# A long convolution with plain float32 operands in place of three float32r products, four filter-tile slots and two input-row buffers

## What is computed

```python
K = 2.0 * jnp.einsum('hn,hnl->hl', Ct, jnp.exp(P)).real      # one filter per head
y = irfft(rfft(u, n=2*L) * rfft(K, n=2*L)[None], n=2*L)[..., :L] + u * D[:, None]
y = y * mask[:, None, :]
# feed-forward, every operand fake-quantised to 8 bits by its rows' maxima:
gate = qlinear(y, w_gate); up = qlinear(y, w_up)
out = x + qlinear(silu(gate) * up, w_down)
```

## Time and profile before

| | us |
|---|---|
| median of 2 runs | 1431.74 |
| lowest, highest | 1426.31, 1437.16 |
| profiled execution | 1423.75 |
| its span | 1422.0 |

### The profile page before, as it was taken

The page is one execution under the profiler, slowest core; times in us unless marked ns, Lnnn a source line. Parts: engine busy times, 40 slices in busy tenths (PEclk is TensorE's granted clock), DMA queues, the critical chain, the costliest instruction groups (busy, mean ns, idle before and its releaser), DMA issues.

```text
span 1422.0 us, 21733 instructions
## 1 busy us (share of the span) xinstructions
PE 1298.7 (91%) x7444; PEld 769.8 (54%) x7444; DVE 1000.0 (70%) x1617; ACT 466.8 (33%) x665; POOL 490.2 (34%) x343
## 2 busy tenths in 40 slices
PE   2378888888888799999999999999999999999998
PEld 0377777878878644444444444444444444444443
DVE  7658889798899766556765676567656765676565
ACT  1145555555565322222222222222222222222222
POOL 2257666676677411222122212221222121212220
PEclk9999999999999899999999999999999999999999
DMA  0087776777787422323322332233223322332222
GB/s 4 8 249 232 217 233 199 235 213 215 252 267 236 164 59 65 63 65 70 90 62 65 70 87 65 65 70 87 65 65 70 85 66 65 70 83 68 65 64 74
DMA packets 137599, 161.58 MB, mean 114 GB/s; under 512 B 101644, under 2 KB 101854, under 8 KB 136286
## 3 DMA queue, kind: packets, MB, share of 16 engines
q1 hardware_dynamic: 137566, 161.16, 40.9%
HBM read 113.28 MB, written 25.49 MB: 98 GB/s over the span
## 4 chain that ended last, share of the span: by engine, by line
PE 64%; DVE 0%; ACT 0%; issue 0%
PE ps_o L1113 22%; PE ps_g L1088 21%; PE ps_u L1088 21%; PE ps_t L1098 0%; ACT h_t L1216 0%; DVE ps_o L1168 0%; DVE res L1171 0%
## 5 line engine op out<-in xcount | busy, mean ns | idle before, releaser
L1242 POOL TENSOR_TENSOR h_int<-h,rounder 128x512 bf16<-128x512 f32 x186 | 186.7, 1025 | 698.2 <-ACT h L1207 695.5
L1088 PE MATMUL ps_g<-wgu,rows 128*128 128x512 bf16 (+1 forms) x1536 | 330.8, 359 | 4.5 <-PEq L377 4.5
L1088 PE MATMUL ps_u<-wgu,rows 128*128 128x512 bf16 (+1 forms) x1536 | 329.0, 357 | 0.0
L1113 PE MATMUL ps_o<-wd,h_t 128*128 128x512 bf16 (+1 forms) x1408 | 319.1, 380 | 0.0
L1201 ACT ACTIVATE g_buf<-g_buf 128x512 f32<-128x512 f32 x192 | 112.3, 585 | 596.3 <-DVE g_buf L1139 596.3
L1139 DVE SCALAR_TENSOR_TENSOR g_buf<-ps_g,sx_all,wide 128x512 f32<-128x512 f32 x192 | 132.3, 689 | 242.4 <-PE ps_g L1088 242.4
L1088 PEld LDWEIGHTS ps_g<-wgu,rows 128*128 128x128 bf16 x1536 | 145.0, 98 | 163.6 <-issue 13.2
L1113 PEld LDWEIGHTS ps_o<-wd,h_t 128*128 128x128 bf16 (+1 forms) x1408 | 134.2, 98 | 178.0 <-issue 34.4
L1088 PEld LDWEIGHTS ps_u<-wgu,rows 128*128 128x128 bf16 x1536 | 146.9, 98 | 151.6 <-issue 0.8
L611 POOL TENSOR_TENSOR t_lo<-t_raw,t_hi 128x1024 fp32r<-128x1024 f32 x64 | 162.5, 2540 | 81.2 <-ACT t_hi L657 81.2
L875 PE MATMUL ps_y<-u_hi,t_hi 128*128 128x512 f32 (+7 forms) x512 | 171.8, 336 | 8.1 <-POOL t_lo L611 3.5
(11 more groups left out here) (149 smaller groups left out, 1024.5 us busy)
## 6 DMA issues: line engine op xcount, KB each, us to landing
t_raw<-k_rev SPq DMA_DIRECT2D x64, 512.0 KB, 5.9
rows<-in_x SPq DMA_DIRECT2D x64, 256.0 KB, 3.9
res<-in_x SPq DMA_DIRECT2D x64, 256.0 KB, 3.9
out_x<-res SPq DMA_DIRECT2D x64, 256.0 KB, 3.2
wide<-in_L_ffn_w_gate SPq DMA_DIRECT2D x22, 512.0 KB, 6.2
wide<-in_L_ffn_w_up SPq DMA_DIRECT2D x22, 512.0 KB, 7.4
wide<-in_L_ffn_w_down SPq DMA_DIRECT2D x8, 1376.0 KB, 7.6
xq_dram<-xq SPq DMA_DIRECT2D x32, 256.0 KB, 5.8
```

Of the source, the lines that this page charges most:

```text
L1088: last = pe.matmul(bank[:, 0:n], xq[:, par, c, :], wgu[:, NC - 1 - c, first + cols.start:first + cols.stop], start=(c == 0), stop=(c == NC ...
L1113: last = pe.matmul(ps_o[o][:], h_t[0:width, c, :], wd[0:width, c, o * W:(o + 1) * W], start=(c == 0), stop=(c == FC - 1))
L1242: pool.tensor_tensor(h_int[:, piece(j)], h[:, par, piece(j)], rounder[:].to_broadcast([P, n]), ALU.subtract).then_inc(h_int_ready, 1)
```

## The change

The operands of the convolution become plain float32: one matmul for each block instead of three, 8 for a head instead of 24, straight from the loaded filter tile `toep` and from the turned input `u`. The splits (`t_high`, `split_t`, `u_low`) and their semaphores are gone; `u_high` becomes `take_u`, the same ScalarE copy out of PSUM into a float32 tile. The filter tiles get four slots (two tiles x two heads) and the input rows a second buffer, so SyncE loads two tiles ahead: filter tile (i+2, hh) is loaded once `convolve(i, hh)` is done, input rows i+2 once tile i has been turned. The first loads are reordered: input rows first, then the filter tiles, and all of tile 1 without a wait.

```diff
-        t_raw = sb("t_raw", [P, 2, L])
-        t_hi = sb("t_hi", [P, 2, L], F32R)
-        t_lo = sb("t_lo", [P, 2, L], F32R)
-        u_hi = sb("u_hi", [P, 2, NC * B], F32R)
-        u_lo = sb("u_lo", [P, 2, NC * B], F32R)
+        toep = sb("toep", [P, 4, L])
+        u = sb("u", [P, 2, NC * B])
+        x_more = sb("x_more", [P, L])
+        x_bufs = (x_rows, x_more)
...
-            load_t(0, 0)
-            load_x(0)
-            load_t(0, 1)
-            for i in range(2):
-                for u in range(2):
-                    load_gu(i, i, u)
-            sp.wait_ge(x_turned, 2)
-            load_x(1)
+            load_x(0, 0)
+            load_t(0, 0, 0)
+            load_t(0, 0, 1)
+            for g in range(2):
+                load_gu(0, 0, g)
+            load_x(1, 1)
+            for g in range(2):
+                load_gu(1, 1, g)
             for hh in range(2):
-                sp.wait_ge(t_lo_done, hh + 1)
-                load_t(1, hh)
+                load_t(1, 1, hh)
...
-                    sp.wait_ge(x_turned, 2 * i + 4)
-                    load_x(i + 2)
-
-                    sp.wait_ge(t_lo_done, 2 * i + 3)
-                    load_t(i + 2, 0)
+                    sp.wait_ge(x_turned, 2 * i + 2)
+                    load_x(i + 2, par)
+
+                    sp.wait_ge(conv_done, 2 * i + 1)
+                    load_t(i + 2, par, 0)
...
-            split_t(0, 0)
-            split_t(0, 1)
...
-                    t_high(i + 1, 0)
-                    u_high(i + 1, 0)
+                    take_u(i + 1, 0)
...
-                if has(i, TILES - 1):
-                    u_low(i + 1, 0)
...
-                pe.wait_ge(x_loaded, 32 * i + 32)
-                pe.wait_ge(u_lo_done, 2 * i + hh - 1)
+            def await_x(i, par):
+                pe.wait_ge(x_loaded[par], 16 * i - 16 * par + 32)
...
-                    parts = ((t_hi, u_hi), (t_hi, u_lo), (t_lo, u_hi))
-                    for k, (t, u) in enumerate(parts):
-                        last = pe.matmul(out[:, dist * B:NC * B], t[:, hh, block_cols], u[:, hh, 0:n],
-                                         start=(dist == 0 and k == 0), stop=(dist == NC - 1 and k == 2),
-                                         skip_group_check=True)
+                    last = pe.matmul(out[:, dist * B:NC * B], toep[:, slot, block_cols], u[:, hh, 0:n],
+                                     start=(dist == 0), stop=(dist == NC - 1), skip_group_check=True)
```

More of the change, by code:

```diff
@@ L507, in _, with load_t, load_x @@
         def _(sp):
-            def load_t(i, hh):
+            def load_t(i, par, hh):
+                slot = 2 * par + hh
                 src = bass.AP(tensor=k_rev.tensor, offset=(2 * i + hh) * KROW, ap=[[1, P], [1, L]])
-                sp.dma_start(t_raw[:, hh, :], src).then_inc(t_loaded[hh], 16)
-            def load_x(i):
+                sp.dma_start(toep[:, slot, :], src).then_inc(t_loaded[slot], 16)
+            def load_x(i, par):
                 for hh in range(2):
-                    sp.dma_start(x_rows[hh * B:(hh + 1) * B, :],
-                                 x[:, bass.ds(2 * i + hh, 1), :].squeeze(1)).then_inc(x_loaded, 16)
+                    sp.dma_start(x_bufs[par][hh * B:(hh + 1) * B, :],
+                                 x[:, bass.ds(2 * i + hh, 1), :].squeeze(1)).then_inc(x_loaded[par], 16)
             def load_gu(i, par, u):
@@ L608, in _ @@
         def _(pool):
[L609 to L612, removed]
             def unround(i, par, k, turned):
@@ L643, in body @@
                     unround(i + 1, 1 - par, 0, pieces(i, 0) + 1)
-                if has(i, TILES - 1):
-                    split_t(i + 1, 1)
                 if not gate_stage(i) and has(i, WEIGHT_ITERS - 1):
@@ L652, in _, with take_u @@
         def _(act):
-            def t_high(i, hh):
-                act.wait_ge(t_loaded[hh], 16 * i + 16)
-                if not isinstance(i, int) or i >= 1:
-                    act.wait_ge(conv_done, 2 * i + hh - 1)
-                act.activation(t_hi[:, hh, :], t_raw[:, hh, :], ACT.Copy).then_inc(t_hi_done, 1)
-            def u_high(i, hh):
+            def take_u(i, hh):
                 act.wait_ge(x_turned, 2 * i + hh + 1)
@@ L694, in _ @@
             for hh in range(2):
-                t_high(0, hh)
-                u_high(0, hh)
+                take_u(0, hh)
             round_gu(0, 0, 0)
@@ L720, in body @@
                 if has(i, TILES - 1):
-                    t_high(i + 1, 1)
-                    u_high(i + 1, 1)
+                    take_u(i + 1, 1)
                 if gate_stage(i):
@@ L776, in scale_w @@
                 dve.wait_ge(w_step, 3 * turn + 3)
-            def u_low(i, hh):
-                dve.wait_ge(u_hi_done, 2 * i + hh + 1)
-                dve.tensor_tensor(u_lo[:, hh, :], ps_x[hh][:], u_hi[:, hh, :].bitcast(F32),
-                                  ALU.subtract).then_inc(u_lo_done, 1)
             def mask_y(i, par, hh):
@@ L814, in quantise_y @@
                 dve.tensor_scalar(xq[:], v, ROUND, ROUND, ALU.add, ALU.subtract).then_inc(xq_ready, 1)
-            for hh in range(2):
-                u_low(0, hh)
             first_max(0, 0)
@@ L838, in body @@
                     max_y(i, par)
-                if has(i, TILES - 1):
-                    u_low(i + 1, 1)
                 if gate_stage(i) and has(i, GU_ITERS - 2):
@@ L851, in _, with turn_x, convolve @@
         def _(pe):
-            def await_x(i, hh):
-                pe.wait_ge(x_loaded, 32 * i + 32)
-                pe.wait_ge(u_lo_done, 2 * i + hh - 1)
-            def turn_x(i, hh):
+            def await_x(i, par):
+                pe.wait_ge(x_loaded[par], 16 * i - 16 * par + 32)
+            def turn_x(i, par, hh):
                 rows = slice(hh * B, (hh + 1) * B)
                 for c in range(NC):
-                    last = pe.transpose(ps_x[hh][:, c * B:(c + 1) * B], x_rows[rows, c * P:(c + 1) * P], ident[rows, rows])
+                    last = pe.transpose(ps_x[hh][:, c * B:(c + 1) * B], x_bufs[par][rows, c * P:(c + 1) * P], ident[rows, rows])
                 last.then_inc(x_turned, 1)
-            def convolve(i, hh):
-                pe.wait_ge(t_lo_done, 2 * i + hh + 1)
-                pe.wait_ge(u_lo_done, 2 * i + hh + 1)
+            def convolve(i, par, hh):
+                slot = 2 * par + hh
+                pe.wait_ge(t_loaded[slot], 8 * i - 8 * par + 16)
+                pe.wait_ge(u_done, 2 * i + hh + 1)
                 if not isinstance(i, int) or i >= 1:
```

26 lines of the change are left out of this document (11 added, 15 removed).

## The result

| | before | after |
|---|---|---|
| median, us | 1431.74 | 1376.66 |
| lowest, highest | 1426.31, 1437.16 | 1376.52, 1376.81 |
| profiled execution | 1423.75 | 1376.52 |
| FFN's first matmul | 499.1 | 451.1 |

The ratio is 0.961 (95% interval 0.955 to 0.968): faster by about 4%. A second measurement of the changed kernel beside the experiments gave 1375.1 us and 0.961 (0.958 to 0.965). The forecast was 1398 and its range began at 1378. On the profiled executions 47 us are gained, and the FFN's first matmul comes 48 us earlier, so all of it lies in the convolution tiles.

What follows compares the result with a forecast made beforehand. A TensorE-VectorE loop before the FFN was taken as the bound. 176.8 + 62c, c = 4.4, ends convolutions at 449.6 us, 38.7 less; minus 5 for waits, 34 less: 1390, or 1398 on the median's scale; range 1378 to 1430.

Steps and rivals of the forecast that it cites:

- the row wait: Gate stretch, TensorE at turn_max: 15.5 us waiting for input rows with one x_rows buffer, claimed to go.
- c: Length of one plain float32 convolution on TensorE: 4.4 us taken, 0.6 us more than an undisturbed one before.
- nothing on top: Low end for a convolution: column passes, start and last record's tail only, 4.2 us.
- the 9 ns a record: Extra time per TensorE record, seen in float32r convolutions; added for 16 records it made a convolution 4.35 us.
- the 0.09 us of L903's pair: L903's second record begins 0.20 us after its first where passes need 0.107; with every record, a convolution takes 5.6 us.
- waits that were not foreseen: Allowance in gate and down iterations: 0.15 us an iteration, 5 us taken off the gain.
- The waits go: TensorE's waits at turn_max, 23.2 us for max_y and 15.5 us for input rows, were both to vanish.
- The path of 4.6 us: From the end of convolve(i, 1) over VectorE to turn_max; TensorE gets there at 5.7 us, 1.1 us to spare.
- rival (a): Gain within 2%: L814 falls behind GpSimd's unround, TensorE waits 0.7 us each gate iteration, 15 us; 1408 to 1413; chance 0.22.
- (b): Slower: plain records each 0.09 us longer, a convolution 5.6 us, 36 us later, 1467; chance 0.08.
- (c): Slower: plain float32 leaves TensorE at the lower clock in convolutions, stage 190 us later, 1620; chance 0.06.
- (d): Nothing moves: the gate loop keeps its 12.9 us for an unseen reason, for instance transfers; chance 0.04.

## Why the prediction was right, and where it was not

**What bounds the kernel: right.** The loop over TensorE and VectorE closed in the named places, and `u_low`, L800 and L814 were the ones to fall. VectorE's gate iteration came to 8.4 us where 8.7 was worked out, L814 to 0.69. What the prediction did not price is how little the buffers bring while VectorE is late: it counted the row wait as a gain of its own, and the float32r kernel with deep buffers lost that wait and won 15 us, while the wait for `max_y` grew from 23.2 to 31.9 us.

**The mis-sized step is c, the length of a convolution.** 4.4 was taken, 4.16 measured, just under even the end called "nothing on top" (4.2). The time of the passes over the columns was right to the hundredth down to 128 columns. What was added was not there: neither the 9 ns a record of the float32r products nor the 0.09 us of L903's pair, which a run of equal records does not show. The last two records come 0.06 us apart. Through the sum:

| term | forecast | measured | difference, us |
|---|---|---|---|
| 62 convolutions | 4.4 each | 4.16 | -14.9 |
| 21 pairs of gate gaps | 2.64 | 2.45 | -3.9 |
| iteration 0 ends | 93.0 | 97.98 | +5.0 |
| iteration 22's gaps | 3.1 | 2.9 | -0.2 |
| down iterations' gaps (8, without the 0.9 for the last scales) | 3.04 | 3.65 | +4.9 |
| last convolution ends | 449.6 | 440.4 | -9.2 |

(the differences are taken before rounding). To these 9 us come the 5 taken off for waits that were not foreseen, of which the gate stage had none, and the scale: the forecast was carried to a median of before 8 us above its profiled execution, while after's two executions lie at 1376.5 and 1376.8. 9 + 5 + 8 is the 21 us between 1398 and 1377, to within 1. With c at 4.16 and no waits taken off, the prediction's own sum and scale give 1378, the edge of its range. That the miss beyond it is small is partly luck: iteration 0 and the down gaps were each 5 us too short, which hid 10 us of the other errors. The slow end of the range was added up too near as well: c = 4.75 and 5 us of waits leave 12 us and not 17.

**Iteration 0: wrong by 5 us.** That the filter tile needs no split was counted; that all first loads are now issued at once, and share the DMA engines, was not. The timeline of TensorE after:

```profile
78.83 6.79 PE L837 MATMUL ps_y<-u,toep 128*128 128x512 f32 x16 [1.96 <-DMA toep<-k_rev]
88.92 0.71 PE L824 MATMUL ps_x<-ident,x_more 64*128 64x64 f32 x8 [3.30 <-DMA x_more<-in_x]
90.65 0.85 PE L855 MATMUL ps_w<-identb,w_int 128*128 128x128 bf16 x8 [1.02 <-POOL w_int L617]
91.29 5.66 PE L837 MATMUL ps_y<-u,toep 128*128 128x512 f32 x16
```

TensorE waits for the rows of tile 1 and then for the first weight tile, and the second convolution behind these waits runs at a granted clock of 0.73 (5.66 us for 4.16).

**"The waits go": right in the gate stage, half right in the down stage.** The path of 4.6 us against TensorE's 5.7 holds for gate tiles. Beside down tiles `quantise_y` takes 2.3 us behind GpSimd's three `unround`, and in five of the eight iterations TensorE waits about half a microsecond for `max_y`; that is rival (a)'s mechanism, in the stage for which it was not drawn up, at some 4 us and not 15. The run with `max_y` ahead of it, where most down iterations take 11.4 us, fits.

**The other rivals.** (b), a pace of 0.09 us more, and (c), the low clock staying, are refused by the timeline and the clock of 1.00. (d) is refused by the result. The rule of the Trainium skill that was weighed ("FP8 and Floating Point Precision", TensorE Precision Notes), four passes for true float32, fits as a count: two records, each as long as two passes. As a price, 5.1 us, it does not: 4.16 was measured. The reason given in the prediction, that narrow matmuls of before were held by their weight loads, makes about 0.5 us of the difference by its own paces; the 9 ns a record that before has and after has not make most of the rest. The prediction's 24 and 16 are all the records of a convolution; those narrow enough to be held are 12 before and 4 after.

**The transfers.** The prediction had the input rows more than an iteration ahead and the filter tiles 18 us early, and neither was waited for after iteration 0. It did not see how much hangs on it: rows that come late cost 30 us, filter tiles that come late 188.

**Where the 53 us lie.** In one order, each step between two measured kernels: deep buffers 15 us (1429 to 1414), plain operands with the side work kept 8 (1414.5 to 1406.5), the second source of the subtraction 20 (to 1386.4), the rest of `split_t` and `t_high` 5 (to 1381.2), `u_low` 5 (to 1376). In another order the shares are others; shallow buffers make plain operands a loss of 130 us. The 8 us are not accounted for: the profiled executions of the two kernels are 3 us apart (1409.8 and 1406.7), and a shorter convolution can hardly be the reason where a longer one cost nothing. The two steps of 5 us rest on two executions of each kernel with work put back, which lie up to 3 us apart.

## What to carry to other kernels

Where two engines wait for each other in turn, price an edit by what it takes from the late one: 27 us of extra TensorE work cost nothing here, 0.5 us on a GpSimd instruction cost 20 to 26, through the VectorE instructions that stand behind it. Before removing a copy, ask what the copy set free: here the split freed the load slot, and without it, with this order of loads, the slots had to double. And when a wait row names a transfer, look at the issuing queue's own waits and at what it issues just in front, since what is late may be an innocent load behind another one.

## What the runs showed of the hardware

A plain float32 matmul of N columns against 128 is two records, each as long as 2N columns at 2.4 GHz take (0.43 us apart at 512, 0.11 at 128); at 64 columns the pair is 0.06 us apart. Eight of 512 to 64 columns take 4.16 us at a granted clock of 1.00.

GpSimd's float32 subtraction of 128 x 1024 takes 1.89 to 2.34 us when both sources are one tile and 2.34 to 2.85 when they are two (means 2.11 and 2.59 to 2.61), beside the same other work. The shortest of each, 1.89 and 2.34, differ by 0.45. The longer ones are held up in their turn: one of 2.81 us starts at 181.86 us while `quantise_y` runs until 182.44.

A VectorE instruction of 128 columns, 0.29 us alone, took 1.54 us on average where its turn came during such a subtraction; the weights' maxima (1.20 to 1.21 us) and the instructions that read PSUM (0.68 and 1.21) kept their lengths.

The input rows' median from issue to landing is 3.7 to 3.8 us where they go out first of a group (before, and after with only the rows late, at DMA shares of 0.72 and 0.76) and 6.5 to 7.0 where a filter tile and a weight tile go out within 2 us in front of them (after, and after with only the filter tiles late, at shares of 0.91 and 0.60). So it goes with the order of the loads and not with the share.
